# Splitting the modulation of a two-layer block: only the first shift and scale in the prelude, the gates later

## What is computed

```python
mod = (silu(c) @ wmod).reshape(2, 6, 1, -1)
sa, ca, ga, sb, cb, gb = (mod[:, i] for i in range(6))
ga = (2 * (ga >= 0) - 1) * maximum(abs(ga), 0.25)      # gb likewise
h = layernorm(x) * (1 + ca) + sa;  x = x + ga * attn(h)
h = layernorm(x) * (1 + cb) + sb;  x = x + gb * ffn(h)
```

## Time and profile before

| | us |
|---|---|
| median of 3 runs | 1101.34 (1100.43 to 1101.61) |
| the profiled execution | 1103.79 |
| its span, the time axis of all rows below | 1101.7 |
| issue of the load of x and of `wmod[0]`, second and third in SP's queue | 1.17 and 1.63 |
| PE, DVE busy over the span | 917.3 (83%), 884.8 (80%) |
| ACT, POOL busy over the span | 616.5 (56%), 458.9 (42%) |
| TensorE's mean granted clock | 0.913 of full |

### The profile page before, as it was taken

One profiled execution on the slowest core, in us unless ns is written; L12 is line 12 of the kernel. 1 busy time (PEld: TensorE's weight loads), 2 busy tenths in 40 slices (PEclk: granted clock), 3 DMA queues, 4 the chain that ended last, 5 costly groups with the idle time before them and its releaser, 6 DMA issues. The chain is left out here.

```text
span 1101.7 us, 16941 instructions
## 1 busy us (share of the span) xinstructions
PE 917.3 (83%) x5454; PEld 611.8 (56%) x5454; DVE 884.8 (80%) x1725; ACT 616.5 (56%) x1313; POOL 458.9 (42%) x432
## 2 busy tenths in 40 slices
PE   5967999999999999998999979885179558737996
PEld 5634667767677776776767735443132342234554
DVE  5489999999999999999889797659979787565443
ACT  2147787777777877786767533223458417713111
POOL 0214876757766555454445462121700320007322
PEclk9689999999999999999999989997589768966999
DMA  6003433343343222122222210001000000021001
GB/s 249 15 29 105 136 119 121 120 120 125 109 142 120 92 88 82 62 78 96 77 77 87 75 71 1 1 1 43 16 1 1 1 1 1 1 83 48 1 1 39
DMA packets 43342, 72.44 MB, mean 66 GB/s; under 512 B 4546, under 2 KB 20930, under 8 KB 42488
## 3 DMA queue, kind: packets, MB, share of 16 engines
q1 hardware_dynamic: 34040, 58.79, 17.0%
q10 hardware_dynamic: 9216, 12.59, 3.1%
HBM read 56.81 MB, written 13.76 MB: 64 GB/s over the span
## 5 line engine op out<-in xcount | busy, mean ns | idle before, releaser
L470 PE MATMUL bank<-hTs,wA 128*128 128x512 bf16 x768 | 180.1, 384 | 1.0 <-DVE u L1476 1.0
L1476 DVE SCALAR_TENSOR_TENSOR u<-bank,chn,u 128x511 f32<-128x511 f32 (+2 forms) x192 | 142.9, 744 | 3.5
L1991 POOL TENSOR_TENSOR xbuf<-xbuf,dec 128x384 f32<-128x384 f32 x64 | 53.2, 832 | 207.2 <-ACT xbuf L1027 167.7
L470 PEld LDWEIGHTS bank<-hTs,wA 128*128 128x128 bf16 x768 | 75.8, 99 | 85.9 <-issue 7.2
L536 PE MATMUL bank<-wB,yb 128*128 128x256 f32 x512 | 121.2, 380 | 0.7 <-DVE acc L1432 0.7
L470 PE MATMUL bank<-hTs,w13s 128*128 128x512 bf16 x372 | 93.7, 400 | 6.3 <-DVE uc L1690 3.0
L536 PEld LDWEIGHTS bank<-wB,yb 128*128 128x128 f32 x512 | 92.5, 190 | 11.1 <-issue 1.1
L2051 POOL TENSOR_TENSOR hfl<-hf 128x512 bf16<-128x512 f32 x44 | 46.0, 1045 | 122.6 <-DVE hf L1700 66.3
L2001 POOL TENSOR_TENSOR yb<-yv,gs 128x512 f32<-128x512 f32 x64 | 81.7, 1276 | 15.2 <-DVE yv L1503 15.1
L609 PE MATMUL bank<-Mm,xbuf 128*128 128x128 f32 x512 | 70.2, 280 | 21.3 <-DVE yv L1503 19.0
L609 PEld LDWEIGHTS bank<-Mm,xbuf 128*128 128x128 f32 x512 | 64.5, 192 | 32.8 <-issue 24.8
(11 more groups left out here) (239 smaller groups left out, 2127.4 us busy)
## 6 DMA issues: line engine op xcount, KB each, us to landing
csb<-csd SPq DMA_DIRECT2D x64, 256.0 KB, 3.5
wA<-in_win SPq DMA_DIRECT2D x32, 256.0 KB, 4.3
wAd<-wA ACTq DMA_DIRECT2D x32, 256.0 KB, 4.1
wA<-wAd SPq DMA_DIRECT2D x32, 256.0 KB, 3.8
wB<-in_wob SPq DMA_DIRECT2D x8, 512.0 KB, 6.2
wBd<-wB ACTq DMA_DIRECT2D x32, 128.0 KB, 3.8
wB<-wBd SPq DMA_DIRECT2D x8, 512.0 KB, 5.5
CB<-in_wbc SPq DMA_DIRECT2D x1, 2048.0 KB, 12.7
```

Source lines behind the costliest of these rows:

```text
L470: last = nc.tensor.matmul(out, wpart(a, kt), hpart(c, kt), start=n == 0, stop=n == 5)
L1476: nc.vector.scalar_tensor_tensor(out=u[:, n % 2, d:S], in0=bank[0][:, 0:S - d], scalar=chn[:, hid, 3 - d:4 - d], in1=u[:, n % 2, d:S], op0 ...
L1991: nc.gpsimd.tensor_tensor(Xw[:, n % 2, :].rearrange("p (t n) -> p t n", n=P), Xdt[:, n % 2, 0:S - P].rearrange("p (t n) -> p t n", n=P), d ...
```

## The change

- **Loads.** Of layer 0's modulation weights only the first shift and scale (chunks 0 and 1) are loaded at the start. The other four chunks come during slot 46 of the scan, into the high half of the groups' weights (`wmr`, in `wbs`), which group 15 read last in slot 45. Layer 1's weights are loaded behind the experts' weights, into `Ex` and `O5`. The groups' weights come in two halves, the first right behind `cst`; `router` is last and has a semaphore of its own. The first four head weights `wA` are loaded in the prelude.
- **Prelude.** `modulation` takes two chunks. `identb`, for which DVE waited for `cst` before its statistics, is copied between the splits. The group weights are split one group at a time, on ACT and on POOL. PE starts group 0 after the two splits of batch 0; steps and decay sums stand between the groups. The clearing of `acc` goes: the first output tile of each row is written, not added. `gates`, `modulation(1)` and `clamp_gates(0)` leave the stage. Decay sums use banks 6 and 7, and the turned sums are copied by ACT.
- **Gates of layer 0.** PE: one gate each at the end of slots 49 and 51 and the second shift and scale at the end of slot 53, all in bank 7. ACT spreads `silu(c)` in slot 48 and copies the gates in slots 50 and 52. DVE clamps in halves at the end of slots 51 and 52, 55 and 57, and takes the second shift and scale in slot 54. `gated_rows(0)` and the three steps behind it each move four slots later, to 54, 56, 58 and 60.
- **Layer 1's modulation.** All of it stands on PE right behind the last expert product of layer 0, before the turned rows. ACT copies and adds the 1, then copies the two gates, before its first `modulated`.

The core of the diff (short helpers that only moved into functions are left out):

```diff
+        GATES = (49, 51, 53)
@@ sync
-            sp.dma_start(wm, io["wmod"][0]).then_inc(q["d_wm0"], 16)
+            sp.dma_start(wm, io["wmod"][0, :, :, 0:2 * D]).then_inc(q["d_wm0"], 16)
             sp.dma_start(cst[:], io["cst"][:, :]).then_inc(q["d_cst"], 16)
+            sp.dma_start(wbf[:, 0:FIRST], io["wbc"][:, 0:FIRST]).then_inc(q["d_wbc"], 16)
...
-            sp.dma_start(wbf, io["wbc"]).then_inc(q["d_wbc"], 16)
+            sp.dma_start(wbf[:, FIRST:G], io["wbc"][:, FIRST:G]).then_inc(q["d_wbd"], 16)
+            for n in range(4):
+                sp.dma_start(wA[:, n, :], io["win"][ORDER[n]]).then_inc(d_wA[n], 16)
-            sp.dma_start(wm1, io["wmod"][1]).then_inc(q["d_wm1"], 16)
...
+                if s == 4 * (B * G - FIRST) - 2:
+                    sp.wait_ge(q["c_proj"], 2 * B * G)
+                    sp.dma_start(wmr, io["wmod"][0, :, :, 2 * D:6 * D]).then_inc(q["d_wmr"], 16)
@@ tensor
-            gates()
-            modulation(1)
...
-            pe.wait_ge(q["wbs_done"], 1)
-            pe.wait_ge(q["hts_done"], 4)
-            pe.wait_ge(q["gm_done"], 4)
+            pe.wait_ge(q["hts_done"], 2)
             first_rows(0)
+            time_steps()
             first_rows(1)
-            for gq in range(FIRST):
-                if gq + 2 < FIRST:
-                    first_rows(gq + 2)
+            first_rows(2)
+            decay_sums()
+            first_products(0)
+            turned_sums()
+            first_rows(3)
+            for gq in range(1, FIRST):
                 first_products(gq)
...
                 scan_slot(s)
+                if s in GATES:
+                    n = GATES.index(s)
+                    if n == 0:
+                        pe.wait_ge(q["d_wmr"], 16)
+                        pe.wait_ge(q["scb_done"], 1)
+                        pe.wait_ge(q["c_evac"], 2 * B * G)
+                    else:
+                        pe.wait_ge(q["gm_done"], n)
+                    rest_of = lambda kt: wmr[:, kt, :]
+                    if n < 2:
+                        gate_rows(rest_of, scb, 3 * n, bank[7])
+                    else:
+                        modulation(0, rest_of, (1, 2), bank[7])
...
+                if L == 0:
+                    pe.wait_ge(q["d_wm1"], 16 * KT)
+                    modulation(1, lambda kt: wm1[kt], (0, 1, 3, 4), bank[2])
+                    pe.wait_ge(q["scb_done"], 2)
+                    for n in range(2):
+                        gate_rows(lambda kt: wm1[kt], scb1, 3 * n + 2, bank[4 + n])
@@ scalar
             first_rows(0)
             first_rows(1)
+            softplus()
+            for g in range(FIRST, G):
+                high_rows(g)
             first_tanh(0)
+            first_rows(2)
+            decays()
+            first_tanh(1)
+            first_evac(0)
+            first_rows(3)
+            first_tanh(2)
+            first_evac(1)
+            first_tanh(3)
...
@@ vector
-                if s == N - 14:
+                if s in (GATES[0] + 2, GATES[0] + 3):
+                    clamp_gates(0, 0, (s - GATES[0] - 2,))
+                if s == GATES[2] + 1:
+                    take_modulation(1, bank[7])
+                if s == N - 10:
                     gated_rows(0)
...
+                if s in (N - 9, N - 7):
+                    clamp_gates(0, 1, ((s - N + 9) // 2,))
...
-            for gq in range(FIRST):
-                first_group(gq)
-            clamp_gates(0)
+            first_taps(0)
+            step_sizes()
+            first_taps(1)
+            step_decays()
+            first_keys(0)
+            decay_rows()
+            first_taps(2)
+            first_keys(1)
+            first_taps(3)
+            first_keys(2)
+            first_keys(3)
@@ gpsimd
-            pool.wait_ge(q["wbs_hi"], 1)
-            nc.gpsimd.tensor_tensor(wbs[:, 1], wbf, wbs[:, 0], ALU.subtract).then_inc(q["wbs_done"], 1)
+            for g in range(G):
+                low_rows(g)
```

More of the change, by code:

```diff
@@ L355, in _ @@
             experts_load(0)
+            sp.wait_ge(q["out_done"], TB * (N // HG))
+            for kt in range(KT):
+                sp.dma_start(wm1[kt], io["wmod"][1, :, kt, :]).then_inc(q["d_wm1"], 16)
             sp.wait_ge(q["xf_done"], B)
@@ L376, in _, with modulation @@
         def _(pe):
-            def modulation(L):
-                w = (wm, wm1)[L]
-                pe.wait_ge(q[f"d_wm{L}"], 16)
-                for n, m in enumerate((0, 1, 3, 4)):
+            def modulation(L, w, chunks, out):
+                for n, m in enumerate(chunks):
                     for ft in range(KT):
@@ L389, in modulation, with gate_rows @@
                 last.then_inc(q["modp_done"], 1)
[L391 to L402 removed]
+            def gate_rows(w, turned, m, out):
+                for b in range(B):
+                    for kt in range(KT):
+                        last = nc.tensor.matmul(out[:, b * D:(b + 1) * D], turned[:, kt * B + b, :],
+                                                w(kt)[:, m * D:(m + 1) * D], start=kt == 0, stop=kt == KT - 1)
                 last.then_inc(q["gmod_done"], 1)
             pe.wait_ge(q["sc_done"], 1)
[L406 removed]
+            pe.wait_ge(q["d_wm0"], 16)
+            modulation(0, lambda kt: wm[:, kt, :], (0, 1), bank[4])
             def turned_rows(n, b, ft, out):
@@ L1148, in heads @@
             def heads():
+                act.wait_ge(q["modp_done"], 3)
+                parts = bank[2][:, 0:16].rearrange("p (c x) -> p c x", c=4)
+                for m in range(4):
+                    last = nc.scalar.activation(mods[:, 1, m].rearrange("p k b -> p (k b)"), parts[:, m, :], ACT.Identity,
+                                                bias=float(m % 2))
+                last.then_inc(q["mods_done"], 1)
+                for n in range(2):
+                    gate_copied(2 + n, bank[4 + n])
                 modulate(2, 1)
@@ L1409, in first_group, with first_keys @@
                 dve.wait_ge(q["c_step"], 6 * gq + 6)
+            def first_keys(gq):
                 keys(gq)
```

278 lines of the change are left out of this document (153 added, 125 removed).

## The result

The changed kernel takes 1085.12 us (median of 4 runs, 1083.07 to 1085.92) against 1100.88 for the kernel before on the same chip: ratio 0.985, 95% interval 0.981 to 0.989. Forecast were 1091.6. The gain is 15.8 us and not 9.8, and it lies just beyond the fast end of the range. Runs of one kernel spread by up to 1% here (the kernel before: 1094.2 to 1104.6 over all chips), so single profiles differ by several microseconds and I compare stages over several profiles where I can.

What follows compares the result with a forecast made beforehand. It took a chain over engines to bound the first 50 us and PE the late scan. Terms -20.6 + 9.0 + 1.8 = -9.8 took execution 1103.79 to 1094.0; the median lies 2.4 lower: 1091.6, range 1087 to 1096.

Steps and rivals of the forecast that it cites:

- The prelude: Start to the scan's first taps: a shorter chain over engines, first taps at 65.4 for 86.09, term -20.6 us.
- Steps 5 and 8: Before the scan: ACT's work from group 1's scale to one tanh, until 39.2; PE's last products to first taps, 65.4.
- The table loads: ACT's two loads between group 1's scale and the first tanh: 1.28 us each by the row, without the skill's drain.
- The gates in the scan: Slots 49, 51 and 53: added work is paid because PE is full, term +9.0 us, ends +4 and +13.
- 7.0 for PE's work: Ends of slots 49, 51 and 53: two gates at 1.8 us each and the second shift and scale at 3.4.
- DVE's 1.0: Scan: four pairs of 128x512 operations and 0.45 for the modulation, 1.0 of 4.7 us paid.
- The clock: Scan: stretches of 2-column matmuls may lower TensorE's clock, taken as 1.0 us lost, from 0 to 2.
- The moved steps: Four steps from slots 50 to 56 to slots 54 to 60: their 3 us stall moves along, same cost.
- The experts' end: Layer 0's last experts: PE's added modulation and gates end 2.6 us late, 0.8 given back, term +1.8 us.
- hidden gates: Rival: PE's added matmuls lie in gaps, the scan pays 2 us, the experts' end nothing: 1083, chance 0.12.

Runs made afterwards that it cites:

- warm-up experiment: Changed kernel with 18 unused matmuls ahead of PE's first modulation: 1086.70 us, ratio 0.986; with 12 more later in the prelude: 1081.72 us, ratio 0.983.
- the kernel with the moved steps: Kernel before with only gated_rows(0) and the three steps behind it moved to slots 54, 56, 58 and 60: 1099.65 us, ratio 0.9998.
- the doubled ones: Changed kernel with PE's two gates and second shift and scale in slots 49, 51 and 53 done twice: 1090.61 us.

## Why the prediction was right and wrong

**The prelude** was right in its mechanism: every step of the chain came in the order forecast, and the first taps within 0.4 us of the time given. Over several executions the term is -17.8 and not -20.6. My rows of before came from an execution in which layer 1's modulation took 6.83 us at the lower clock; in the same code it also took 5.44 and 3.63, and the groups began 2.2 and 4.1 us earlier. Steps 5 and 8 of the prediction add up to 39.05 and 65.1 by their own terms, where it writes 39.2 and 65.4; that is small beside this. The table loads cost what the row said: Ln begins 0.02 us behind its load. The Trainium skill's drain of 1.38 us (ScalarE: Activation LUTs, What ACT_TABLE_LOAD costs) isn't seen here, in neither of the two loads.

**The gates in the scan** are the step that failed: +9.0 was forecast, +4.1 measured. The term was 7.0 for PE's work, 1.0 for DVE and 1.0 for the clock. The runs give 4.8, 1.0 and -1.7.

PE's work was sized too high. In the prediction's words, "the second shift and scale is 16 records, half of 6.83: 3.4"; it took 1.84 and cost 1.6, for both rows of a modulation that I had were of PE at its slower rate (6.83 at a granted clock of 0.50; 6.96 as PE's first work after idling). The warm-up experiment shows the latter by itself. The Trainium skill says it too (TensorE: Matmul & The Clock Gate, Part 1: The HAM clock gate): "the default state is throttled, and activity releases the throttle", and the traces agree, 3.55 us without and 1.92 with work ahead. I did not weigh it; it would have halved the 3.4. A gate I gave 1.8 and it cost 1.6.

DVE's 1.0 was right. The changed kernel without PE's gates still has the added work of DVE and ACT. Against the kernel with the moved steps its slots ending at heads 50, 52, 54 and 58 are 0.14, 0.13, 0.44 and 0.31 longer.

The clock is the larger miss, 2.7 of the 4.9, and it had the wrong sign. I took 1.0 as the price of added slow stretches; instead some stalls got shorter. Of 14 stalls in seven profiles with the gates in the scan 7 kept a clock of 1.00, of 12 without them none did (that kernel without PE's gates included), and one that keeps it is 1.7 us shorter. The two stalls together took 23.9 us on average in five profiles before and 22.2 in six of the changed kernel. Why PE's added work two slots ahead goes with a kept clock is open: PE's wait is as long in both cases (3.17 and 2.56 us), the windows show the clock, and no run here isolates its cause.

**The moved steps** were priced right, at nothing.

**The experts' end** had the right sign and the wrong reason. PE's work took 3.50 + 5.38 = 8.9 us and not 12.5, again by the modulation's rate, and fitted the wait; the 0.8 paid is DVE's clamp in halves (4.7 us for 3.9), which I had counted as waiting work.

**Not foreseen**: 1.3 us between heads 0 and 49, in code that hardly changed (an average; the single profiles overlap). It is the two slots that end at heads 18 and 19: 18.9 to 19.2 us in all six profiles of kernels with the old order, 17.6 with the changed kernel's, and 18.3 to 18.5 where I changed its prelude again in three of the variants. A DVE operation there meets POOL or doesn't, by what came before: it started 0.16 us behind POOL's instruction in the first of these rows and 0.02 ahead of it in the second. The same operation before and after:

```profile
232.62 1.65 DVE L1389 SCALAR_TENSOR_TENSOR BT<-thx,ug 128x512 f32<-128x512 f32 x1
```

```profile
211.47 0.68 DVE L1479 SCALAR_TENSOR_TENSOR BT<-thx,ug 128x512 f32<-128x512 f32 x1
```

That the time came within 6.5 us is in part luck: the prelude brought 2.8 less than forecast, while the gates cost 4.9 less, the experts' end 1.0 less, and the rest 2.2 less, of which only the 1.4 of the two slots above is traced. Of the rivals, hidden gates (1083, given 0.12) names the nearest time, but not the mechanism: the gates are paid, and the doubled ones too. Runs differ by up to 1% and not by the 0.1% that I read from three.

## What to carry to other kernels

Price an operation of PE by a row in which PE had been busy just before, or give both rates as the ends; a row from the start of a kernel can be twice the later price. Before adding work to a full engine, look a slot or two further for the place where it waits: the second shift and scale and the gate `gb` cost 1.6 us each in full slots, and moved ahead of two stalls they cost nothing there and the stalls got shorter. And before taking a long piece off an engine, ask which other wait ends at the same time, for 9.6 us of gates were covered by one step of DVE.
